# A first table of tiles from the counts of four chunks, in a one-core RWKV block with routed experts

## The reference, cut to what matters

```python
xn = _ln(x, ln1_g, ln1_b); xp = _shift(xn)
k = (xn * mix_k + xp * (1 - mix_k)) @ Wk          # v and sigmoid r likewise
wkv = _wkv(k, v, time_decay, time_first)          # a linear recurrence over the 256 positions
x = x + r * wkv @ Wo
yn = _ln(x, ln2_g, ln2_b); yp = _shift(yn)
kk = square(relu((0.5 * yn + 0.5 * yp) @ Wfk)); rr = sigmoid(yn @ Wfr)
x = x + rr * (kk @ Wfv)
...
scores = einsum('btd,ed->bte', x, gate_w)         # x: layernorm of the above
topk_scores, topk_idx = top_k(scores, 2); topk_probs = softmax(topk_scores)
h12 = einsum('btd,ehd->bteh', x, w12); hidden = silu(h12[..., :256]) * h12[..., 256:]
y = sum over the two chosen experts of prob * (hidden @ w3)
```

## Time and profile before

| | |
|---|---|
| median of 3 runs | 346.33 us |
| the profiled execution's own time | 345.16 us |
| its span in the profile | 343.1 us |
| PE busy | 265.0 us (77%) |
| DVE busy | 248.9 us (73%) |
| POOL busy | 213.8 us (62%) |
| ACT busy | 197.3 us (58%) |
| mean granted TensorE clock | 0.928 of full |

### The profile page before, as it was taken

One profiled execution on the slowest core, in us unless ns is written; L12 is line 12 of the kernel. 1 busy time (PEld: TensorE's weight loads), 2 busy tenths in 40 slices (PEclk: granted clock), 3 DMA queues, 4 the chain that ended last, 5 costly groups with the idle time before them and its releaser, 6 DMA issues.

```text
span 343.1 us, 6748 instructions
## 1 busy us (share of the span) xinstructions
PE 265.0 (77%) x1697; PEld 206.3 (60%) x1698; DVE 248.9 (73%) x790; ACT 197.3 (58%) x413; POOL 213.8 (62%) x227
## 2 busy tenths in 40 slices
PE   0588599998969879676839534899999999999600
PEld 0234266675737547464636332699999999999600
DVE  3079998999799997998825448166666666666784
ACT  2547478787857668565536213367777776766100
POOL 5224456357858878587687677346666666666690
PEclk9999899999989999996998955999999999999955
DMA  7920000001100111011011214433333333333686
GB/s 262 447 65 2 0 0 2 31 4 46 48 31 31 38 48 39 32 39 54 26 39 54 70 40 118 93 88 91 94 93 90 92 87 88 86 95 107 232 262 228
DMA packets 22405, 29.07 MB, mean 85 GB/s; under 512 B 4317, under 2 KB 15583, under 8 KB 22128
## 3 DMA queue, kind: packets, MB, share of 16 engines
q1 hardware_dynamic: 14832, 13.45, 13.7%
q0 software_dynamic: 4352, 8.47, 7.6%
q10 hardware_dynamic: 3200, 6.90, 5.5%
HBM read 15.09 MB, written 12.14 MB: 79 GB/s over the span
## 4 chain that ended last, share of the span: by engine, by line
issue 30%; DVE 26%; POOL 20%; DMA 5%; PE 3%; SPq 1%; DVEq 1%; POOLq 1%; ACT 1%
POOL res_d L443 11%; POOL rows_d L418 5%; DVE st L827 4%; DVE rden L888 2%; DVE den L878 2%; DVE num L882 2%; DVE xm L932 2%; DVE mv L834 2%; DMA o_all<-res_d 2%; DMA res_d<-yo,result_row 2%; POOL rs L367 2%; POOL gated L382 1%; DMA rows_d<-rows,pos 1%; DVE ekv L877 1%; DVE x L902 1%
## 5 line engine op out<-in xcount | busy, mean ns | idle before, releaser
L443 POOL DMA_INDIRECT res_d<-yo,result_row x72 | 71.2, 988 | 39.1 <-issue 29.6
L418 POOL DMA_INDIRECT rows_d<-rows,pos x64 | 66.3, 1037 | 22.6 <-issue 22.0
L801 PE MATMUL p_up<-xgT,w_up 128*128 128x128 f32 x576 | 70.2, 275 | 0.0
L801 PEld LDWEIGHTS p_up<-xgT,w_up 128*128 128x128 f32 x576 | 67.2, 192 | 0.0
L1058 DVE SCALAR_TENSOR_TENSOR gate_h<-th,p_up 128x512 f32<-128x512 f32 x36 | 24.7, 687 | 38.5 <-ACT th L605 38.5
L620 ACT ACTIVATE w_up<-w_exp 128x512 f32 x72 | 41.3, 622 | 10.7 <-issue 10.2
L716 PE MATMUL p_up<-ysum,w_sb 128*128 128x512 f32 x64 | 34.7, 650 | 4.5 <-POOL ysum L397 4.5
L605 ACT ACTIVATE th<-p_up 128x512 f32<-128x512 f32 x36 | 21.5, 597 | 27.6 <-PE p_up L801 27.6
L728 PEld LDWEIGHTS p_f<-wfv_half,kk 128*128 128x128 f32 x256 | 30.9, 192 | 4.7 <-issue 4.3
L728 PE MATMUL p_f<-wfv_half,kk 128*128 128x128 f32 x256 | 32.0, 277 | 0.0
L888 DVE RECIPROCAL rden<-den 128x512 f32<-128x512 f32 x8 | 26.7, 3343 | 0.0
(11 more groups left out here) (153 smaller groups left out, 548.2 us busy)
## 6 DMA issues: line engine op xcount, KB each, us to landing
xg<-rows_d SPq DMA_DIRECT2D x72, 65.0 KB, 1.9
o_all<-res_d SPq DMA_DIRECT2D x16, 256.0 KB, 4.7
w_exp<-experts ACTq DMA_DIRECT2D x1, 3072.0 KB, 17.0
x_all<-x SPq DMA_DIRECT2D x10, 256.0 KB, 2.3
out<-x_all ACTq DMA_DIRECT2D x8, 256.0 KB, 2.4
x_all<-x SPq DMA_DIRECT2D x1, 1536.0 KB, 15.7
res_d<-yo,result_row POOLq DMA_INDIRECT x72
rows_d<-rows,pos POOLq DMA_INDIRECT x64, 2.4
```

The costliest lines, as they stand in the source:

```text
L418: pool.indirect_dma_start(out=rows_d[:, :], out_offset=bass.IndirectOffsetOnAxis(ap=row, axis=0), in_=rows_of[is_last(c)][:, t, k, :], in_ ...
L443: pool.indirect_dma_start(out=res_d[:, :], out_offset=bass.IndirectOffsetOnAxis(ap=row, axis=0), in_=yo[u][:, n, :], in_offset=None, bound ...
L801: mm = pe.matmul(p_up[u % 2][:, n, h * P:(h + 1) * P], w_up[u % 2][:, n, h * P:(h + 1) * P], xgT[u % 2][:, n, :], start=True, stop=True)
```

## The change

A product on PE (`count_early`) takes the counts of the first four chunks. DVE makes from them a first table (`early_table`) of 24 slots, each a full tile of rows of chunks 0 to 3. SP loads all twelve pairs behind its step for chunk 5, each into a buffer of its own, which lies in the room of `o_all`. Their steps on PE, ACT, DVE and POOL are woven by hand-written lists into turns 8 to 12 of the pipelines (`(turn, n)` is behind step n of the list in that turn); what is left of them comes behind the pipelines. Pairs 0 to 5 all use the second pair of banks `p_up` and one part of `p_r`. The second table (`late_table`, inside the DVE's pipeline) has 48 slots for the other tiles. Its loads wait until the rows of all chunks and all pads are written; `late_rows` and the test by pair go. POOL's scatter takes the row numbers from `xg` itself, without DVE's copy, and the load into a buffer waits for the scatter from it. All loops are unrolled. The fillers on PE (`warm_up(3)`, `warm_up(4)`) go.

```diff
-EARLY = 3
+EARLY_CHUNKS = 4
+LAST_SINGLE = 6
+EARLY_PAIRS = 12
+EARLY_SLOTS = 2 * EARLY_PAIRS
+LATE_SLOTS = SLOTS - EARLY_SLOTS
+LATE_PAIRS = PAIRS - EARLY_PAIRS
...
+TURNED_AT = {('m', 5): 1, ('y', 7): 2, ('m', 6): 6, ('m', 7): 11}
...
+        o_raw = sb("o_raw", [P, TOPK * TILES * D])
+        o_all = o_raw[:, :].rearrange("p (k t d) -> p k t d", k=TOPK, t=TILES)
+        for q in range(EARLY_PAIRS):
+            xg.append(o_raw[:, q * 2 * ROW:(q + 1) * 2 * ROW].rearrange("p (n w) -> p n w", n=2))
+            yo.append(o_raw[:, TILES * D + q * 2 * D:TILES * D + (q + 1) * 2 * D].rearrange("p (n d) -> p n d", n=2))
...
+        def up_of(q):
+            return 1 if q < LAST_SINGLE else (q - LAST_SINGLE) % 2
+        def down_of(q):
+            if q < LAST_SINGLE:
+                return p_r[:, 2 * P:4 * P]
+            return (p_tok, p_f)[(q - LAST_SINGLE) % 2][:, 0:2 * P]
...
+            def load(q):
+                sp.load(row_numbers, slot_row[0:1, 2 * q:2 * q + 2])
+                b = buffer_of(q)
+                if q >= EARLY_PAIRS + BUFS:
+                    sp.wait_ge(S[f"scattered{b}"], 32 * ((q - EARLY_PAIRS) // BUFS))
+                loaded = S[f"early_loaded{q}" if q < EARLY_PAIRS else f"xg_loaded{b}"]
+                for n in range(2):
+                    first_row = sp.snap(row_numbers[n], min_val=0, max_val=E * REGION + (IDLE - 1) * P)
+                    sp.dma_start(xg[b][:, n, :], rows_d[bass.ds(first_row, P), :]).then_inc(loaded, 16)
+            def load_early(q):
+                if q == 0:
+                    sp.wait_ge(S["early_row"], 1)
+                    sp.wait_ge(S["dispatched_early"], 16 * EARLY_CHUNKS * TPC * TOPK)
+                load(q)
+            pipeline(sp, [(keep, 0)], {(5, 0): [(load_early, q) for q in range(EARLY_PAIRS)]})
 
 
...
+            sp.wait_ge(S["dispatched"], 16 * (CHUNKS - 1 - EARLY_CHUNKS) * TPC * TOPK)
+            sp.wait_ge(S["last_dispatched"], 16 * TPC * TOPK)
+            sp.wait_ge(S["idle_filled"], 16)
             sp.wait_ge(S["table_row"], 1)
...
+            sp.wait_ge(S["pad_filled"], 16 * E)
+            for q in range(EARLY_PAIRS, PAIRS):
+                load(q)
+            sp.wait_ge(S["early_scattered"], 32 * EARLY_PAIRS)
...
+            def scatter(q):
...
+                    row = xg[b][:, n, D:D + 1].bitcast(U32)
                     pool.indirect_dma_start(
                         out=res_d[:, :], out_offset=bass.IndirectOffsetOnAxis(ap=row, axis=0),
-                        in_=yo[u][:, n, :], in_offset=None, bounds_check=q + RESULTS, oob_is_err=False)\
-                        .then_inc(S[f"scattered{u}"], 16)
-
-            rounds(pool, [(scatter, 0)], 0)
+                        in_=yo[b][:, n, :], in_offset=None, bounds_check=RESULTS, oob_is_err=False)\
+                        .then_inc(S["early_scattered" if q < EARLY_PAIRS else f"scattered{b}"], 16)
+            pipeline(pool, [(add_ffn, 3), (shift_sum, 2), (add_residual, 2), (ln3_power, 3), (last_ln1_power, 2),
+                            (dispatch_first, 4), (ln2_power, 1), (dispatch_second, 4), (gate_sums, 0)], {(9, 0): [(scatter, 0)], (9, 5): [(scatter, 1)], (9, 7): [(scatter, 2), (scatter, 3)],
+                      (10, 0): [(scatter, 4)]})
...
+            def expert_weights(q):
+                if q == 0:
+                    act.wait_ge(S["early_w"], 1)
+                    act.wait_ge(S["experts_in"], 16)
+                if q == EARLY_PAIRS:
+                    act.wait_ge(S["table_w"], 1)
+                act.load(loaded, slot_w[0:1, 2 * q:2 * q + 2])
+                after(act, "up_done", q - 1)
+                for n in range(2):
+                    first_col = act.snap(loaded[n], min_val=0, max_val=(E - 1) * EW)
+                    last = act.activation(w_up[q % 2][:, n, :], w_exp[:, bass.ds(first_col, 2 * H)], ACT.Copy)
+                last.then_inc(S["weights_copied"], 1)
...
+                     {(9, 17): [(expert_weights, 0)], (10, 0): [(turned_rows, 0)], (10, 1): [(tanh, 0)],
+                      (10, 3): [(expert_weights, 1)], (10, 5): [(turned_rows, 1)],
+                      (10, 12): [(tanh, 1), (expert_weights, 2)],
+                      (10, 15): [(turned_rows, 2), (expert_weights, 3)], (10, 17): [(tanh, 2)],
+                      (10, 19): [(turned_rows, 3), (turned_rows, 4), (expert_weights, 4)],
+                      (11, 0): [(tanh, 3), (turned_rows, 5)], (11, 4): [(expert_weights, 5)], (11, 6): [(tanh, 4)],
+                      (11, 7): [(turned_rows, 6)], (11, 10): [(expert_weights, 6)], (11, 12): [(tanh, 5)],
+                      (11, 15): [(expert_weights, 7), (turned_rows, 7), (tanh, 6), (expert_weights, 8), (turned_rows, 8)],
+                      (11, 19): [(turned_rows, 9), (turned_rows, 10)], (12, 3): [(expert_weights, 9)],
+                      (12, 15): [(expert_weights, 10)], (12, 19): [(tanh, 7), (turned_rows, 11)]})
+            rest([(turned_rows, -1), (tanh, 0), (expert_weights, -2)], (12, 8, 11))
...
-                if is_last(c):
-                    after(pe, "trr_ready", CHUNKS)
-                    warm_up(3, p_tok)
...
+            def count_early(c):
+                if c == EARLY_CHUNKS:
+                    pe.wait_ge(S["seen_ready"], EARLY_CHUNKS + 1)
+                    pe.wait_ge(S["exp_done"], CHUNKS)
+                    pe.matmul(p_k[:, 0:E], ones[:, :], seen[:, :], start=True, stop=True).then_inc(S["early_counts"], 1)
...
+            def up(q):
 
                 after(pe, "xgT_ready", q + 1)
+                after(pe, "weights_copied", q + 1)
+                if q == 0:
+                    pe.wait_ge(S["early_steps"], 1)
+                    pe.wait_ge(S["ekv_ready"], CHUNKS)
+                if q == LAST_SINGLE:
+                    pe.wait_ge(S["relu_done"], FB * CHUNKS)
+                elif q <= LAST_SINGLE + 1:
+                    after(pe, "hid_ready", min(q, LAST_SINGLE))
+                else:
+                    after(pe, "hid_ready", q - 1)
+                b = up_of(q)
                 for n in range(2):
                     for h in range(2 * H // P):
-                        mm = pe.matmul(p_up[u % 2][:, n, h * P:(h + 1) * P], w_up[u % 2][:, n, h * P:(h + 1) * P],
-                                       xgT[u % 2][:, n, :], start=True, stop=True)
+                        mm = pe.matmul(p_up[b][:, n, h * P:(h + 1) * P], w_up[q % 2][:, n, h * P:(h + 1) * P],
+                                       xgT[q % 2][:, n, :], start=True, stop=True)
...
+            def down(q):
+                pe.load(loaded, slot_w[0:1, 2 * q:2 * q + 2])
                 first_col = [pe.snap(value, min_val=0, max_val=(E - 1) * EW) for value in loaded]
                 after(pe, "hid_ready", q + 1)
-                after(pe, "yo_ready", q - 1)
+                if q < LAST_SINGLE:
+                    after(pe, "yo_ready", q)
+                    for name, count in DOWN_GUARDS.get(q, ()):
...
+                     {(9, 4): [(turn_rows, 0)], (9, 5): [(up, 0)], (9, 8): [(turn_rows, 1)], (9, 12): [(up, 1)],
+                      (9, 13): [(down, 0)], (9, 17): [(turn_rows, 2)],
+                      (10, 0): [(up, 2), (down, 1), (turn_rows, 3)],
+                      (10, 2): [(turn_rows, 4), (up, 3), (down, 2), (turn_rows, 5)], (10, 7): [(down, 3)],
+                      (10, 8): [(up, 4)], (10, 11): [(turn_rows, 6)], (10, 12): [(up, 5)],
+                      (10, 14): [(turn_rows, 7)],
+                      (10, 18): [(up, 6), (down, 4), (turn_rows, 8), (up, 7), (down, 5), (turn_rows, 9), (up, 8), (turn_rows, 10)],
+                      (11, 10): [(turn_rows, 11)]})
+            rest([(turn_rows, -1), (up, 0), (down, 1)], (12, 9, 6))
 
...
+            def early_table(c):
+                if c != EARLY_CHUNKS:
+                    return
+                some = EARLY_SLOTS
+                dve.wait_ge(S["early_counts"], 1)
+                early_link(dve.tensor_scalar(part[:, :], p_k[:, 0:E], 1.0 / P, (1 - P) / (2.0 * P), ALU.mult, ALU.add))
+                early_link(dve.tensor_scalar(full[:, :], part[:, :], WHOLE, -WHOLE, ALU.add, ALU.add))
+                dve.tensor_tensor_scan(full_cum[:, :], ones_e[:, :], full[:, :], 0.0, ALU.mult, ALU.add)
+                early_link(dve.tensor_scalar(full_coef[:, :], full[:, :], -float(P), float(REGION), ALU.mult, ALU.add))
+                early_link(dve.tensor_tensor(past[:, 0:some, :], spread_e(slot_no[:, 0:some], some),
+                                             spread_s(full_cum[:, :], some), ALU.is_ge))
+                dve.tensor_tensor(past_rows[:, 0:some, :], past[:, 0:some, :], spread_s(full_coef[:, :], some), ALU.mult)
+                early_link(dve.tensor_reduce(slot_e[:, 0:some], past[:, 0:some, :], mybir.AxisListType.X, ALU.add))
+                early_link(dve.tensor_reduce(slot_first[:, 0:some], past_rows[:, 0:some, :], mybir.AxisListType.X, ALU.add))
```

(81 more changed lines are left out.)

271 lines of the change are left out of this document (135 added, 136 removed).

## The result

The changed kernel took 343.44 us in the median of 4 runs (343.0 to 343.89), the kernel before 346.37 us in 4 runs of the same session (345.4 to 346.85). The ratio is 0.9926, with a 95% interval of 0.9903 to 0.9948: 2.9 us faster, where 7.7 were forecast. The time is inside the range (329.5 to 348), and 4.8 us above the value.

A forecast was written before the change was run, and what follows sets the result against it. PE was taken to set the second stage's pace, with POOL only 0.35 us a pair behind. Terms 12.1 - 2.6 - 0.5 - 1.3 = 7.7 us took 346.3 to 338.6 us; range 329.5 to 348.

The forecast's parts named there:

- pair 12: First late pair: its transposes on PE come at 237.5 against 249.61, a gain of 12.1 us.
- ring: Reuse of six buffers, each load waiting for the scatter: losses of 2.6 us at pair 18 and 0.5 after.
- end: After the last pairs: SP's reading of the first half of results moves some 4 us later, loss 1.3 us.
- The front's shift, "+14.8": Chunk 7's chain: ln3_power(7) moves from 196.62 to 211.4, and the dispatches behind it shift by 14.8 us.
- 5.5 of the 19.1 us added: PE, turns 9 and 10: waits absorb about 5.5 of 19.1 us added, so gated_ffn(7) moves to 204.
- I take 0: DVE's early table ahead of rw(7): being held behind POOL's sums could cost 1.5 us at most; taken as 0.
- All of that lies under the wait to 235.1: Behind the count: the late table and 8.1 us of PE work finish before chunk 7's dispatches land at 235.1.
- The stall at pair 18: First reused buffer: POOL's backlog brings the load in at 257.5, PE wants it at 254.9; loss 2.6 us.
- The steady ring: After pair 18: one cycle takes 17.4 us for six pairs, just PE's own 17.4; loss 0.5 us.
- The pace of 2.90: Second stage on PE: 2.90 us a pair, apart from a wait at pair 18.
- instruction fetch: Slower rival: with all loops unrolled, ten more fetches exposed on the chain give 350 us; chance 0.04.
- waits for `hid` above 1 us: Slower rival: PE stands before up 1 to 6, six stands of 2.0 us, 12 us, giving 350.6; chance 0.14.

The follow-up runs named there:

- e11: e9 with all scatters on POOL behind the pipelines, none of the early pairs' woven in: 347.11 us, ratio 1.0021.
- e12: e1b with the scatter of pair 0 moved behind ln3_power(6) on POOL: 337.79 us, ratio 0.9772.
- e4: The changed kernel with tanh(7) and gate_hidden(7) moved ahead of the count, before the late table: 341.69 us, ratio 0.987.
- e5: The changed kernel with rw(7) ahead of the early table on DVE and pair 0's first weights one step later on ACT: 343.75 us, ratio 0.9953.
- e6: The changed kernel, six buffers, with DVE's copy of row numbers restored for late pairs, so loads wait for yo only: 338.96 us, ratio 0.9801.
- e9: e1b with the edit of e4 added: 339.68 us, ratio 0.9826.
- e10: e9 with two unread products more in PE's wait before pair 12: 338.59 us, ratio 0.9787.
- e1b: The changed kernel with eight buffers in place of six for the late pairs: 337.51 us, ratio 0.9754.
- c2: e1b measured again, unchanged, in the session of e12: 338.62 us, ratio 0.9793.
- c1: The changed kernel measured again, unchanged, in the session of e1b, e5 and e6: 342.26 us, ratio 0.9898.
- e3: The kernel before with all loops unrolled and nothing else changed: 344.47 us, ratio 0.9969.
- e2: The changed kernel without weaving, all woven steps of the twelve early pairs put behind the pipelines: 349.77 us, ratio 1.0106.

## Why the prediction was right in direction and wrong in size

In the two profiled executions the sum (pair 12, ring, end) came out as 7.1 - 4.9 - 1.3 = 0.9, in place of 12.1 - 3.1 - 1.3 = 7.7.

**The front's shift, "+14.8", was 17.8** (3.0 of the missing 6.8). The forecast let PE's waits take 5.5 of the 19.1 us added, and had `gated_ffn(7)` at 204. PE was in fact busy all of 191 to 206, and `gated_ffn(7)` stood at 205.4 to 207.8 in eleven traces of kernels with the weaving, the lowest two in e11 and e12, where `var` was not held. So the step that failed is that PE's waits would take 5.5 of the 19.1 us. Three parts can be told. The waits took less of the work than thought: even there it is 1.4 and 1.9 us late. With `var` held and up 3 at full clock it stood at 206.28 to 206.97 (e4, e5, e6, e9, e10), 0.4 to 1.1 us later than in e12. And where PE's wait before up 3 was 2.15 us, as here, in e1b and in c2, up 3 took 3.48 to 3.63 us in place of 2.02, and `gated_ffn(7)` stood at 206.97 to 207.62. c1 had a wait of 1.94 us, a fast up 3 and still 207.82, with a front that was 3 us late from the start.

Counted from `gated_ffn(5)` the order is clearer: 51.1 to 51.8 us in the three traces with the wait of 2.15 us, 49.0 to 49.1 in the six with `var` held and up 3 at full clock (c1 among them), 48.2 in e12 and 49.5 in e11. But in the three 0.5 to 1.2 us of this are lost before `gated_ffn(6)` already, for a reason that no run tells. So of these last two parts only the direction is shown, as executions of one kernel differ by as much.

**"I take 0" for the early table was wrong in mechanism, and its effect is not isolated.** The forecast kept 1.5 us as the cost if table operations were held behind POOL's sums; `rw(7)` ended 2.1 us later. It was an operation with one input of 8 numbers that was held. e5 took this delay away without a gain, but put the table, and with it the rows of pair 0, behind `rw(7)`. The rule of the Trainium skill (SBUF — State Buffer, "SBUF: two separate sides"), an exclusive lock on the shared port pair, agrees with the trace by the 5.07 us that end with POOL's last sum, and was a better guide than my "0". It names a second kind beside operations with two SBUF inputs, those in a mode that uses both ports; that `full` is one of these is my reading, and no run tells it.

**"All of that lies under the wait to 235.1" failed** (2.0 of the missing 6.8). The 8.1 us of PE's work were right in number at full clock. PE did it in 18.6 us, 223.85 to 242.48: it waited 6.1 us for `hid` of pairs 7 and 8, and the same products took 13.3 us by their rows, some 5 us more, at the lower clock. `hid(7)` stands behind the late table on DVE. `hid(8)` waits for its tanh, and on ACT this stands behind the copy `xgT` of pair 11, which waits for up 9:

```profile
234.73 0.38 ACT L612 ACTIVATE xgT<-p_tr 128x256 f32<-128x256 f32 x1 [7.33 <-PE p_up L831]
235.01 0.59 ACT L606 ACTIVATE th<-p_up 128x512 f32<-128x512 f32 x1
```

So PE does up 9, only then ACT the tanh of pair 8, and PE stands for it before down 8. The rows of pair 12 were in by about 240.5, as e4 shows. But e4, e9 and e10 also show that this term was never to be had in full: without PE's own lateness it waits for the rows, and pays for the wait at the lower clock.

**The ring, "2.6" and "0.5", was 4.9** (1.8 of the missing 6.8). The stall at pair 18 was 0.8, since PE itself came 5.0 later; "POOL starts 252.8, load in 257.5" was 255.81 and 260.65. The steady ring was mis-sized. From pair 18 to 35 the trace has (314.05 - 260.70) / 17 = 3.14 us a pair, so six take 18.8 us, not 17.4. The landing of the scatter was as forecast (2.2 to 2.3). The load took 1.9 to 3.2 from issue to landing with about 0.7 for the issue: from 279.07, where the scatter at 276.74 has landed, to PE at 282.84 are 3.8 us where the forecast had 2.35. The rest of the excess, 0.4, lies ahead of the scatter (13.05 us from the transposes of pair 19 at 263.69 to 276.74, forecast 10.6 + 0.8 + 1.27 = 12.67). I took 1.9 from the median of the earlier trace rows, whose row itself had a maximum of 3.2, for two loads issued one after the other of which the second counts. A ring whose sum equals PE's pace to the tenth has no slack, and each excess of a term is paid once every six pairs, with no way to gain it back. e1b and e6 take the whole term away and give 3.3 to 4.75 us.

**The end, "1.3", held in number; its cause did not.** From pair 35 to the end of the span are 342.2 - 314.05 = 28.15 us, before 343.1 - 316.27 = 26.83. SP's reading of the first half did move. In the trace before, after, and of e6 it starts at:

```profile
314.42 3.94 SPq L310 DMA_DIRECT2D o_all<-res_d  x8
...
315.31 4.50 SPq L324 DMA_DIRECT2D o_raw<-res_d  x8
...
306.76 13.54 SPq L325 DMA_DIRECT2D o_raw<-res_d  x13
```

That is 1.85 us ahead of pair 35's transposes before and 1.26 behind them after, 3.1 later against the stage. But in e6, where load 35 waits for `yo` again, it is 1.9 ahead of pair 35's 308.68, and the end takes 28.4 us all the same; in e1b it is 2.4 ahead and the end takes 28.6. So the later reading is not shown to cost the 1.3, the right number is in part luck, and what makes the end longer stays open.

**The pace of 2.90** held to the third digit (66.66 / 23), as did 1.27 us a scatter on POOL, without a gap from 235.39 to 260.92 (forecast to about 266).

Of the rivals, instruction fetch is refuted (e3), waits for `hid` above 1 us were real only at one place in the front (2.15 us) and two behind the count (6.1 us), and the gain of weaving is 6 to 7 us (e2). With the ring repaired the medians give what had been forecast, 337.5 and 338.6 us (e1b, c2), 8.1 and 7.1 below the kernel before. The sum does not: in the trace of e1b it is 6.6 us at pair 12, nothing for the ring and 1.8 lost at the end (338.3 - 309.71 = 28.6), 4.8 in all. That execution took 340.12 us, 2.6 above its median, and the trace before was 1.2 below its own; so that the medians meet the forecast does not show that its sum was right. e1b has the lowest time of all versions; e6, e9, e10, e12 and c2 are within 2.2 us of it, in other sessions but for e6.
